# Pooled attention: the softmax denominators from sums of two key tiles, made on GpSimd and VectorE

## What is computed

```python
x = x + attention(group_norm(x))          # first block
x = x + conv3x3(relu(xn * mask))          # second block, xn = group_norm(x)
# attention, upper 128 channels: 4 heads of 32; queries are the 1024 pixels,
# keys and values the 256 means of 2x2 pixels
attn = softmax(q @ k.T / sqrt(32))        # 1024 x 256 a head
lo   = (attn @ v) @ l_proj_w + l_proj_b
# lower 128 channels: attention within each 2x2 window, then h_proj
```

## Time and profile before

| what | us |
|---|---|
| runs | 347.5, 350.32, 352.98 |
| median | 350.32 |
| span of the profiled execution | 347.5 |
| that execution's own time | 347.5, the lowest of the three |
| TensorE busy | 315.2 (91%) |
| VectorE busy | 272.5 (78%) |
| ScalarE busy | 148.8 (43%) |
| GpSimd busy | 83.0 (24%) |

### The profile page before, as it was taken

One profiled execution on the slowest core, in us unless ns is written; L12 is line 12 of the kernel. 1 busy time (PEld: TensorE's weight loads), 2 busy tenths in 40 slices (PEclk: granted clock), 3 DMA queues, 4 the chain that ended last, 5 costly groups with the idle time before them and its releaser, 6 DMA issues.

```text
span 347.5 us, 4162 instructions
## 1 busy us (share of the span) xinstructions
PE 315.2 (91%) x1566; PEld 222.3 (64%) x1566; DVE 272.5 (78%) x488; ACT 148.8 (43%) x189; POOL 83.0 (24%) x46
## 2 busy tenths in 40 slices
PE   0879968999979999999799999999799999999995
PEld 0566344267866663688567744888388727877884
DVE  4996668769999586889989767799887847897572
ACT  2442548464490843554047855351165423031300
POOL 2088513440436020003910200008600200202000
PEclk9999968899989999999999999999999999999999
DMA  8779500009700000099011200197001000101002
GB/s 276 276 102 140 228 5 0 2 1 134 94 0 4 2 1 2 0 130 159 1 63 41 82 1 2 35 128 128 4 0 62 0 0 5 58 0 62 0 0 121
DMA packets 12068, 20.38 MB, mean 59 GB/s; under 512 B 2065, under 2 KB 8081, under 8 KB 11793
## 3 DMA queue, kind: packets, MB, share of 16 engines
q1 hardware_dynamic: 12048, 20.13, 28.2%
HBM read 7.93 MB, written 4.19 MB: 35 GB/s over the span
## 4 chain that ended last, share of the span: by engine, by line
PE 58%; DVE 23%; ACT 8%; issue 6%; POOL 3%; DMA 2%; SPq 0%; DVEq 0%; POOLq 0%
PE slot L1113 29%; PE cps L1145 15%; PE slot L1189 7%; DVE l_max L848 3%; PE cps L1113 3%; DVE mask L784 3%; PE cps L1189 2%; ACT probs L563 2%; POOL probs L379 2%; DVE v_lo L814 1%; DMA xy<-x 1%; PE slot L1392 1%; ACT xn_hi L452 1%; ACT p_w L608 1%; DVE xn L740 1%
## 5 line engine op out<-in xcount | busy, mean ns | idle before, releaser
L1145 PE MATMUL cps<-v_hi,cw_hi 128*128 128x512 f32 (+1 forms) x144 | 57.6, 400 | 3.5 <-DVE v_lo L814 2.9
L1145 PE MATMUL cps<-v_hi,cw_lo 128*128 128x512 f32 (+1 forms) x144 | 57.9, 402 | 0.0
L1145 PE MATMUL cps<-v_lo,cw_hi 128*128 128x512 f32 (+1 forms) x144 | 56.4, 392 | 0.0
L379 POOL TENSOR_TENSOR probs<-q_w,k_w 128x1024 f32<-128x1024 f32 x14 | 32.9, 2376 | 79.5 <-DVE rw L777 72.3
L848 DVE TENSOR_REDUCE l_max<-slot 128x4 f32<-128x1024 f32 x32 | 37.1, 1216 | 5.9 <-PE slot L1113 5.9
L563 ACT ACTIVATE probs<-slot 128x1024 f32<-128x1024 f32 x32 | 31.4, 1021 | 16.0 <-PE slot L1113 15.9
L1145 PEld LDWEIGHTS cps<-v_hi,cw_hi 128*128 128x128 f32 x144 | 27.4, 191 | 12.7 <-issue 5.2
L1145 PEld LDWEIGHTS cps<-v_hi,cw_lo 128*128 128x128 f32 x144 | 27.4, 190 | 7.4 <-issue 2.2
L1145 PEld LDWEIGHTS cps<-v_lo,cw_hi 128*128 128x128 f32 x144 | 27.4, 190 | 5.0
L362 POOL TENSOR_TENSOR mask<-rw 128x1024 f32<-128x1024 f32 x8 | 15.2, 1912 | 56.6 <-DVE rw L777 56.6
L1113 PE MATMUL slot<-xn_hi,w_hi 128*128 128x512 f32 (+1 forms) x68 | 27.3, 401 | 1.1 <-ACT xn_hi L452 1.1
(11 more groups left out here) (197 smaller groups left out, 635.0 us busy)
## 6 DMA issues: line engine op xcount, KB each, us to landing
xy<-x SPq DMA_DIRECT2D x8, 512.0 KB, 6.6
out<-xy SPq DMA_DIRECT2D x8, 512.0 KB, 2.6
qs<-probs SPq DMA_DIRECT2D x12, 256.0 KB, 5.8
qs<-probs SPq DMA_DIRECT2D x24, 128.0 KB, 8.3
raw_cw<-conv_w SPq DMA_DIRECT2D x2, 1152.0 KB, 6.4
ks<-probs SPq DMA_DIRECT2D x12, 128.0 KB, 6.9
probs<-h_qkv SPq DMA_DIRECT2D x2, 192.0 KB, 3.8
probs<-l_kv SPq DMA_DIRECT2D x2, 128.0 KB, 3.7
```

The costliest lines, as they stand in the source:

```text
L379: nc.gpsimd.tensor_tensor(product(b, j).rearrange("p (n w) -> p n w", n=NW), q_w[:].rearrange("p (n w) -> p n w", n=NW), k_w[:, j * G:(j + ...
L1145: ins = nc.tensor.matmul(cps[:, pos % 2, y0 * WT:y1 * WT], (cw_hi, cw_hi, cw_lo)[part][:, k, pos, dy + 1, o * P:(o + 1) * P], (v_hi, v_lo, ...
```

## The change

- New tile key_sum (128 partitions, 4 heads, 1024 pixels), laid over qs.
- For each head the two key tiles of exponentials are added: key_sum[h] = probs[2h] + probs[2h + 1]. GpSimd does heads 0 and 1 of image 0 (between the turning of the weights and their low parts) and heads 0, 1 and 2 of images 1 to 3 (heads 0 and 1 ahead of its sum of line 427, head 2 behind it). VectorE does heads 2 and 3 of image 0 and head 3 of the others, ahead of normalisation(b + 1, 0).
- TensorE: the values come first (16 matmuls, as before), then the denominators as 8 matmuls on key_sum, which wait for both engines' sums, then window_out. Before, the denominators were 16 matmuls and stood first. In image 3 window_out still comes first.
- VectorE: residual(b, 0, 1) moves from ahead of the product into q_w to behind split_input.
- ScalarE: xn_hi waits for the denominators of both halves and no longer for the values.
- Fillings: before the projection of q_w 13 convolution matmuls in place of 8 in images 2 and 3, and 11 in place of 7 in image 1, where each of the last four score tiles is followed by 1 in place of 2.

```diff
-REST = (4, 3, 5, 3, 4, 8)
+REST = (4, 3, 5, 3, 4, 13)
-REST_1 = (1, 1, 2, 2, 2, 7)
+REST_1 = (1, 1, 2, 2, 1, 11)
...
+        key_sum = nc.alloc_sbuf_tensor_at("key_sum", [P, HEADS, HW], F32, offset=qs_at)
...
+        def vector_heads(b):
+            return range(HEADS - (2 if b == 0 else 1), HEADS)
+        def pool_heads(b):
+            return range(HEADS - len(vector_heads(b)))
+        def key_sums(engine, h):
+            return engine.tensor_tensor(key_sum[:, h], probs[:, h * MT], probs[:, h * MT + 1], ALU.add)
...
+                for h in pool_heads(0):
+                    sum_of_keys(0, h)
...
+            def sum_of_keys(b, h):
+                pool.wait_ge(st_exp, b * LT + (h + 1) * MT)
+                key_sums(nc.gpsimd, h).then_inc(dsum_pool, 1)
...
-                    pool.wait_ge(pv_ready, b * NW + 2)
-                    nc.gpsimd.tensor_tensor(pv[0], pv[0], pv[1], ALU.add).then_inc(pv_pool, 1)
+                    for h in pool_heads(b):
+                        if h == 2:
+                            pool.wait_ge(pv_ready, b * NW + 2)
+                            nc.gpsimd.tensor_tensor(pv[0], pv[0], pv[1], ALU.add).then_inc(pv_pool, 1)
+                        sum_of_keys(b, h)
...
-                act.wait_ge(lpv_pe, b)
+                act.wait_ge(lden_pe, b * 2)
...
+                for h in vector_heads(b):
+                    dve.wait_ge(st_exp, b * LT + (h + 1) * MT)
+                    key_sums(nc.vector, h).then_inc(dsum_dve, 1)
                 if not last:
                     normalisation(b + 1, 0)
...
-                if not last:
-                    residual(b, 0, 1)
...
                 split_input(b + 1)
+                residual(b, 0, 1)
                 residual(b, 1, 2)
...
+            def denominators(b):
+                pe.wait_ge(dsum_pool, sums_by(b, pool_heads))
+                pe.wait_ge(dsum_dve, sums_by(b, vector_heads))
+                for half in range(2):
+                    for h in range(HEADS):
+                        last = mm(slot[2][HD * h:HD * (h + 1), half], cst[:, C_ONE:C_ONE + HD],
+                                  key_sum[:, h, halves(half)], True, True)
+                    last.then_inc(lden_pe, 1)
...
-                by_head(2, lambda t, h: cst[:, C_ONE:C_ONE + HD], lden_pe)
+                pooled_values()
+                denominators(b)
                 if not last:
                     window_out()
-                by_head(0, lambda t, h: lv[:, t, HD * h:HD * (h + 1)], lpv_pe)
```

More of the change, by code:

```diff
@@ L141, in build @@
         v_w = sb("v_w", [P, HW])
+        qs_at = nc.sbuf_base
         qs = sb("qs", [P, HEADS, HW], F32R)
+        key_sum = nc.alloc_sbuf_tensor_at("key_sum", [P, HEADS, HW], F32, offset=qs_at)
         ks = sb("ks", [P, HEADS, G], F32R)
@@ L224, in build @@
         lden_pe, blocks_c, fold_c = sem("lden_pe"), sem("blocks_c"), sem("fold_c")
+        dsum_pool, dsum_dve = sem("dsum_pool"), sem("dsum_dve")
         lpv_pe, lnorm = sem("lpv_pe"), sem("lnorm")
@@ L230, in build, with sums_by @@
         conv_pe, conv_out = sem("conv_pe"), sem("conv_out")
+        def vector_heads(b):
+            return range(HEADS - (2 if b == 0 else 1), HEADS)
+        def pool_heads(b):
+            return range(HEADS - len(vector_heads(b)))
+        def sums_by(b, heads):
+            return sum(len(heads(i)) for i in range(b + 1))
+        def key_sums(engine, h):
+            return engine.tensor_tensor(key_sum[:, h], probs[:, h * MT], probs[:, h * MT + 1], ALU.add)
         def means_at(b, i):
@@ L1237, in pooled_scores, with pooled_values @@
                 last.then_inc(st_pe, 1)
-            def by_head(s, lhsT, ready):
+            def pooled_values():
                 for half in range(2):
@@ L1243, in by_head @@
                         for h in range(HEADS):
-                            last = mm(slot[s][HD * h:HD * (h + 1), half], lhsT(t, h), probs[:, h * MT + t, halves(half)],
+                            head = slice(HD * h, HD * (h + 1))
+                            last = mm(slot[0][head, half], lv[:, t, head], probs[:, h * MT + t, halves(half)],
                                       t == 0, t == MT - 1)
-                    if ready is lden_pe or half == 1:
-                        last.then_inc(ready, 1)
+                last.then_inc(lpv_pe, 1)
+            def denominators(b):
[6 more added lines that the diff above has]
+                    last.then_inc(lden_pe, 1)
             def window_scores_of(b, j, to):
```

## The result

The kernel after takes 358.61 us (median of 4 runs, 357.75 to 361.95), the kernel before 350.31 us. The ratio is 1.0267, with an interval of 1.022 to 1.0314: slower by more than 2%. The profiled execution has a span of 355.9 us, 8.4 more than before, and took 357.75 us itself.

A forecast was written before the change was run, and what follows sets the result against it. TensorE was taken as the main bound, with the chain leaving it for VectorE and ScalarE. Net terms for images 0 to 3, +1.7 + 4.6 + 0.65 + 1.35 = +8.3 us, gave 358.6 us on the median; range 347 to 362.

The forecast's parts named there:

- The gain of 2.85 us without blocking: All images: fewer denominator matmuls and the new order gain 1.75, 0.8 and 0.5 us in images 2, 3, 1; image 0 loses 0.2.
- rival "no blocking": All images: GpSimd's additions cost VectorE nothing, or only off the path; 347.5 us, chance 0.12.
- Image 1's softmax, 4.1 us: Image 1's window softmax: VectorE's L873 and L876 wait behind two GpSimd additions, delaying TensorE; cost 4.1 us.
- a rival with a chance of 0.1 and a price of 3.5 us: Image 1: a TensorE stall brings another clock dip, with following work at the lower level; +3.5 us, 362.1 us, chance 0.1.
- Images 2 and 3, 2.4 and 2.15 us: Convolution tiles: L805 or L806 waits for GpSimd, delaying ScalarE's casts and p_w; cost 2.4 and 2.15 us before gains.
- idle 2 us ahead of the first values: Sign in images 2 and 3: TensorE would show a 2 us gap ahead of the first values.
- Image 1's tail, +0.5 us: End of image 1: head 2's addition holds L997 for 2.4 us, taking the 0.5 us gain and 0.5 more.
- Image 0, +1.7 us: Image 0's window sums: L993 waits behind GpSimd's additions, counted as 1.5 us, plus 0.2 us lost without blocking.
- the 0.2 us in it: Image 0 without blocking: product 0.7 us sooner, but residual later, with ScalarE's moments queued behind it; loss of 0.2 us.
- The start, 0: Start to image 0's third exponential: no change forecast, 0 us.
- Span and time: Whole kernel: the profiled execution's 347.5 us was taken as its span, with nothing around it, giving 355.8 us after.
- GpSimd busy, 109 us: Sign on GpSimd: busy time of 83.0 us plus eleven additions of 2.4 us gives 109 us.

The follow-up runs named there:

- e4: Kernel after, but GpSimd's additions wait for VectorE's window softmax in image 1 and its low parts of convolution tiles in images 2 and 3; 349.99 us.
- e5: Kernel after, with each of GpSimd's eleven additions replaced by three fills of the same tile, which write but read nothing; 347.21 us.
- e10: e9 with image 0 also in its old order (denominators, window_out, values, residual ahead of the product); 348.06 us, ratio 0.9914 to before.
- e1: Kernel before with GpSimd's eleven additions put in, their sums unused and the 16 denominator matmuls kept; 359.14 us.
- e6: e4 with three of image 0's heads added on VectorE and one on GpSimd; 349.59 us.
- e9: e7 without key-tile additions in image 0, whose 16 denominator matmuls read the exponentials, behind the values; 350.2 us.
- e7: e6 with VectorE also adding head 2 of images 1 to 3, so GpSimd adds only heads 0 and 1 there; 349.77 us.

## Why the prediction was right

The time came out at 358.61 against 358.6 us, and the span of the profiled execution at 355.9 against 355.8. The mechanism was right: additions on GpSimd hold VectorE at the places named, most of all in the softmax of image 1, and the loss is larger than the gain on TensorE. That the numbers are so close is luck. Dips of the clock in B, C and E brought some 3.3 us that were in no term of the sum, the start gave back 1.5 us, and without those dips B to G come to 4.4 us (C and E taken from e4) where the forecast had 6.6. By the terms:

- **The gain of 2.85 us without blocking.** Right on the whole. TensorE's projection after image 2 comes 2.03 us sooner (1.8 forecast). In e4, with the clock at 1.00 in all three, C, E and G are 0.2, 1.5 and 0.8 us shorter (0.5, 1.75 and 0.8 forecast); in after the 1.5 us of E shrank to 0.84 with a clock of 0.97. e5, where no new instruction blocks another, took 347.21 us where the rival "no blocking" stood at 347.5.
- **Image 1's softmax, 4.1 us.** Right in place and size: 3.85 us, in two turns, one for each addition. It was the cast that waited for the second turn, not the subtraction behind it. The cost of the stretch was still under-sized, since the clock fell behind that stall: +5.84 us. That case stood apart as a rival with a chance of 0.1 and a price of 3.5 us; it happened, at 2 us.
- **Images 2 and 3, 2.4 and 2.15 us.** Right in the stretch, wrong in the step. I had one of L805 and L806 wait, and ScalarE's cast with it. In fact VectorE's tile instructions went through and GpSimd waited 2.4 us; the cast and the second pair of exponentials came on time (5.56 us behind the first, 5.55 before). What waited were the two low parts behind it, 3.8 us together. So TensorE did not idle 2 us ahead of the first values, as forecast (0.30 us in image 2, as before), but 1.43 and 1.09 us ahead of the third, for VectorE's late product. Of the 3.8 us 1.73 and 1.32 us show in the stretches; before, VectorE had idled 1.78 and 2.17 us behind the low parts, and that took most of the rest.
- **Image 1's tail, +0.5 us.** Head 2's addition held VectorE's head sum (2.73 us in place of 1.22) and not L997, since VectorE's own instruction was under way when GpSimd's fell due: 1.5 us in place of 2.4. The step that failed is that this wait lies on the path: in e4 the head sum took 2.79 us and the stretch was 57.60 us, and in e5, where nothing waited, 57.58. The +0.40 us of after is the clock (0.97); e4 and e5, at 1.00, are 0.2 us shorter than before.
- **Image 0, +1.7 us.** L994 waited 2.17 us and L993 0.2, in place of L993 alone with 1.7 (of which the sum has 1.5); with everything 1.5 us earlier at the start, L993 was ahead of the second addition. The stretch is +2.26, but A varies by about as much between profiles of the same work (e10 against before), so the size of this term, and of the 0.2 us in it, is not shown.
- **The start, 0.** It was 1.5 us shorter by a better clock (0.98 against 0.95), which made up for part of the clock in image 1.
- **Span and time.** I had taken the two as equal. The profiled execution of after took 1.85 us more than its span, and the later runs of before some 2.2 us more (349.79 us for a span of 347.5). The forecast on the median does not hang on it, since it adds the 8.3 us to a median.
- **GpSimd busy, 109 us.** It was 118.0, since GpSimd waits too, which the forecast had left out.

The Trainium skill, page "SBUF — State Buffer", section "Who interferes with whom", carried the right reading: VectorE with two SBUF inputs waits for a GpSimd instruction that reads SBUF and not for one that only writes (e5 against after). By the same section a cast can be one of those that contend; here it took 2.25 us beside an addition, 0.23 us with nothing beside it (e4) and 0.30 us beside a fill.

## What to carry to other kernels

An idle GpSimd is not free to use. Each of its additions, which read SBUF, held up VectorE's instructions with both inputs in SBUF, and here a cast as well, while VectorE's products with one input from PSUM went through; a 0.29 us step on the path became 2.1 us. Before moving work there, list VectorE's instructions that fall due in its time by their inputs. A wait that starts GpSimd behind them costs nothing if its result is wanted later: one such wait took 5.8 us off stretch B here, 3.85 of blocking and 2 of clock. And a halved count of matmuls is worth only what the stage's last waiter leaves: of 7.1 us of matmuls about 2.5 arrived (C, E and G of e4).

## What the runs showed that was not expected

- Who waits is not settled by who fell due first. In images 2 and 3 VectorE's tile instructions kept GpSimd out for 2.4 us (an addition of 4.81 us), although GpSimd's addition fell due ahead of most of them. In the softmax, where each VectorE instruction waits by semaphore for the one ahead of it, GpSimd's second addition got its turn right behind L903. But GpSimd also got a turn between the two low parts of image 2, and between L1023 and L1024 of image 0, which follow each other as closely as the tile instructions. No run varied this, and the rule stays open.
- A stall of 4.18 us on TensorE was followed by a granted clock of 0.79 over its stretch of 16.1 us, where the same stretch without the stall (before, and again e4) had 1.00. It added 2 us to the 3.85 that the stall itself lasted. In e1 the same stall was followed by 0.89 over the stretch and added 0.85 us.
- Which stretch has a dip of the clock differs from kernel to kernel even where the work is the same (C of e6 and e9 is 0.6 us longer than that of e4, e7 and e10, and their clock rows have a slice of digit 8 there). Changes of under a per cent can't be read from one profile of this kernel; outside A, stretches agree where their granted clocks do.
